# Attention over sixteen images: projections in even units, transposes in odd ones, statistics earlier

## The chip, the core and the metric

The kernel runs on one core of one Trainium2 chip. The metric is the device time of one execution in microseconds; the median of three runs before the change is 4224.94 us (4224.76 to 4225.04).

## What is computed

For each of 16 images of 1024 tokens and 512 channels: a group norm over 32 groups of 16 channels with scale and offset, SiLU, a projection to queries, keys and values (512 x 1536), attention with 8 heads of 64, an output projection (512 x 512) with bias, and the image itself added.

```
xn  = silu(group_norm(x, gn_scale, gn_offset))
q, k, v = split(xn @ w_qkv)            # 8 heads of 64, q scaled by 64 ** -0.5
out = softmax(q @ k.T) @ v             # per image and head
return out @ w_out + b_out + x
```

All of it is float32 in the reference. The kernel keeps that accuracy with pairs of float16 numbers: a value is split into a high part (rounded to float16) and a remainder (low part), and a product takes three passes (high x high, high x low, low x high).

## The kernel before

**Units.** One image is 64 units `v`, four steps `s` of 16 units `u`; a step is a pair of heads, a unit is 512 queries of one head against 256 keys. In unit `v` PE makes the scores (four matmuls of 512 columns, L1018 and L1019), ACT the exponentials twice (L591 in float32, L594 in float16), DVE (even `v`, L795) or POOL (odd `v`, L492) their remainder, and PE the product with V of unit `v - 2` (L1052). ACT takes the sums out of PSUM every fourth unit (L602), DVE and POOL normalise them (L802, L803, L499).

**Score blocks ("tops").** Before the exponentials of a head can start, each query's maximum is needed. `top_use` makes a block of raw scores with one matmul on 64 of the 128 rows (L943), DVE takes its maximum (L741), and after eight blocks a shift is computed (L731, L733) and spread over the rows by a further block (L951, L746). A unit holds three, two or one block (`TOPS_PER_W`). They go through two PSUM banks: PE's block n waits until DVE has drained block n - 2.

**Side uses.** Everything else that PE does shares one PSUM bank, SD, and is put into units by the table `SIDE`, one dictionary per step: "qk" (a half of Q or K of the next step's pair), "v" (128 tokens of V of the next image), "out" (128 tokens of the output of the image before), each 12 matmuls of 512 columns (L929); "xt" (128 tokens of the next image's x transposed, four float32 transposes, L992), "ot" (a half of the attention output of a pair transposed, L986), and "mean" and "var", two small matmuls that average channel statistics over groups (L996, L999). A side use waits until the one before it is drained: ACT writes the high part (L553, L558, L569) or the copy (L565), DVE the remainder (L682, L687, L694) or, for "out", adds bias and image (L699). ACT and DVE drain a side use at the start of the next unit (`side_before`).

**Order inside a unit on PE** (`step`, L1057 to L1082): scores; `place[0]` score blocks; the product with V; blocks up to `place[1]`; the first half of a projection ("qk", "v", "out" are split, `SPLIT`); blocks up to `place[2]`; the second half, or a whole transpose; the other blocks. `TOP_PLACES` depends on whether the unit before held a projection ("late"): (1, 2, 3) if not, (2, 2, 3) if so, and one block fewer in each eighth unit.

**The next image's statistics.** SP loads x (`load_x`, two buffers) once PE has transposed the block two before. When all eight "xt" are drained, DVE takes `bn_stats` over the channels (`channel_stats`, eight of 512 tokens, L756) and joins them (`aggregate`, L762); "mean" and "var" follow on PE with a few small DVE instructions each (L705 to L722), POOL makes three Newton steps for the reciprocal root (`newton`, twelve small instructions, L466 to L473), DVE the coefficients (`coefficients`, L770 to L780). Then the SiLU, eight pieces: ACT in units 7 to 14 of step 2 (`silu_parts`, L579 and L581), DVE one unit later (`silu`, L785 and L788), POOL the remainder (`low_xn`, L479). A "qk" of step 3 and a "v" wait for these remainders.

**SP's queue.** In order: stores of outputs, loads of the second half of the residual rows (each waits for a store), loads of x, and in unit 10 of each step `place`: 12 DMAs that copy Q and K of the next pair to where the scores read them (L385).

The loops over images run on each engine by itself; the first two steps and the last image stand outside the loop, and after the last unit an epilogue does what is left ("ot" of pairs 2 and 3 and eight "out").

Of the kernel before, what the change touches and what calls it, by code (L numbers as in the profile page):

```python
# [78 lines left out]
def top_uses(step, u, last=False):  # L79
# [3 lines left out]
    if last and step == 3 and hh == 1:  # L83
# [14 lines left out]
    {0: "qk", 1: ("ot", 2, 0), 2: "qk", 3: ("ot", 2, 1), 4: "qk", 5: "qk", 6: ("ot", 3, 0),  # L98
     7: ("ot", 3, 1), 8: "out", 10: "out", 12: "out", 13: "out", 14: "out", 15: "out"},
    {0: "qk", 1: "xt", 2: "qk", 3: "xt", 4: "qk", 5: "xt", 6: "qk", 7: "xt", 8: "xt", 9: "xt", 10: "xt",  # L100
     11: "xt", 13: "out", 14: "out"},
    {0: ("ot", 0, 0), 1: ("ot", 0, 1), 2: "mean", 3: "qk", 4: "var", 5: "qk", 6: "qk", 7: "qk", 12: "v",
     13: "v", 14: "v"},
    {0: "qk", 1: ("ot", 1, 0), 2: "qk", 3: ("ot", 1, 1), 4: "qk", 5: "qk", 8: "v", 10: "v", 12: "v",
# [10 lines left out]
def side_uses(step, u, first=False, last=False):  # L115


    kind = SIDE[step].get(u)
    if kind is None:
        return []  # L120
    if kind[0] == "ot":
        return [] if first and step == 0 else [kind]

    n = sum(k == kind for at, k in SIDE[step].items() if at < u)
    if kind == "qk":
        return [] if last and step == 3 else [("qk", (step + 1) % 4, "qk"[n % 2], n // 2)]
    if kind == "out":
        return [] if first else [("out", n + (list(SIDE[0].values()).count("out") if step == 1 else 0))]
    if last:
        return []  # L130
    if kind == "v":
        n += list(SIDE[2].values()).count("v") if step == 3 else 0
    return [(kind, n)]
# [34 lines left out]
EPILOGUE = [("ot", pair, half) for pair in (2, 3) for half in (0, 1)] + [("out", t) for t in range(TB)]  # L168
# [42 lines left out]
def conv_attention(nc, x, gamma, beta, w_qkv, w_out, b_out, out):  # L211
# [4 lines left out]
    with ctx:  # L216
# [132 lines left out]
        def _(sp):  # L349
# [36 lines left out]

            def step(b, s, cnt, first=False, last=False):
                filled = []
# [3 lines left out]
                for u in range(16):  # L392
# [10 lines left out]
                    if s == 0 and u == 9 and not last:  # L403
# [38 lines left out]
        def _(pool):  # L442
# [63 lines left out]
            def step(b, s, first=False, last=False):  # L506
                for u in range(16):
# [5 lines left out]
                    if s == 2 and u == 5 and not last:  # L513
# [133 lines left out]
        def _(dve):  # L647
# [164 lines left out]
            def step(b, s, cnt, first=False, last=False):  # L812
                for u in range(16):
# [16 lines left out]
                    if s == 1 and u >= 12 and not last:  # L830
                        channel_stats(b + 1, 2 * u - 24, cnt)
                        channel_stats(b + 1, 2 * u - 23, cnt)
                    if s == 2 and not last:
                        if u == 1:


                            aggregate(b + 1)
                        if u == 6:
# [301 lines left out]
```

## Time and profile before

| | |
|---|---|
| median of three runs | 4224.94 us |
| profiled execution | 4226.06 us |
| its span (first to last instruction) | 4224.3 us |
| PE busy | 3989.4 us (94%) |
| DVE busy | 3128.5 us (74%) |
| ACT busy | 2835.4 us (67%) |
| POOL busy | 1626.7 us (39%) |
| mean granted TensorE clock | 0.981 |

The page gives, for one execution, how long each engine was busy and who waited for whom. PE's busy time counts a matmul from its start to its modelled end, so matmuls that follow each other every 0.22 us appear with some 0.38 us each and overlap; the distance between starts says what one costs. The granted clock is 1.00 when TensorE runs at 2.4 GHz and 0.50 at 1.2 GHz. A unit is recognised by its first score matmul (L1018), and a step by sixteen of them.

### The profile page before, as it was taken

Reading aid. Unit: us, or ns where it says so; the run is one execution under the profiler, and the core shown is the slowest. Engines: PE = TensorE matmul, PEld = TensorE weight load, DVE = VectorE, ACT = ScalarE, POOL = GpSimd, SP = SyncE. Lnnn points to the kernel's source line nnn. Section 1 sums busy time; section 2 is a strip of 40 time slices with the busy share of each in tenths; the row PEclk is TensorE's granted clock in tenths of the full one; section 3 lists DMA queues with packets and bytes.
Section 4 is the critical chain, followed back from the end, with each engine's and each line's share of the span. In section 5 each row is a group of like instructions: output and inputs, shape, how many; then the busy total and the mean of one; then the engine's idle time right before and its main releaser. Section 6 shows DMA issues by size and latency. Waiting matters only on the chain.

```text
span 4224.3 us, 94104 instructions
## 1 busy us (share of the span) xinstructions
PE 3989.4 (94%) x32844; PEld 2038.7 (48%) x32844; DVE 3128.5 (74%) x5216; ACT 2835.4 (67%) x3202; POOL 1626.7 (39%) x1226
## 2 busy tenths in 40 slices
PE   3899999999999999999999999999999999999997
PEld 1444545445454444545445454454544545454443
DVE  5686777868777687776877778687776877778774
ACT  2576676767667676676766767676676766767664
POOL 1243343433434343343433434333343433434333
PEclk8999999999999999999999999999999999999999
DMA  2111212122031120311112121220311203121121
GB/s 77 28 49 36 71 31 76 31 61 61 16 91 31 51 56 19 88 31 56 51 43 68 28 76 33 59 61 16 91 31 51 56 24 83 31 59 49 39 60 33
DMA packets 119394, 211.50 MB, mean 50 GB/s; under 512 B 19536, under 2 KB 19536, under 8 KB 118992
## 3 DMA queue, kind: packets, MB, share of 16 engines
q1 hardware_dynamic: 118992, 205.86, 18.0%
q8 instruction: 286, 4.69, 0.5%
q14 instruction: 116, 0.95, 0.1%
HBM read 71.57 MB, written 33.55 MB: 25 GB/s over the span
## 4 chain that ended last, share of the span: by engine, by line
PE 71%; issue 12%; DVE 9%; POOL 4%; ACT 3%; DVEq 1%; DMA 0%; SPq 0%; ACTq 0%; POOLq 0%
PE SD L929 31%; PE PV L1052 13%; PE TP L943 10%; PE ST L1018 6%; PE ST L1019 6%; DVE Pl L795 2%; DVE mx L741 2%; POOL Pl L492 2%; PE SD L992 1%; POOL xn L479 1%; PE TP L951 1%; ACT QK_hi L553 1%; PE SD L986 1%; ACT Ph L594 1%; DVE Q L746 1%
## 5 line engine op out<-in xcount | busy, mean ns | idle before, releaser
L741 DVE TENSOR_REDUCE mx<-TP 128x1 f32<-128x512 f32 x2048 | 1349.3, 684 | 346.7 <-PE TP L943 338.1
L591 ACT ACTIVATE P<-ST,cns 128x1024 f32<-128x1024 f32 x1024 | 1142.6, 1116 | 532.6 <-PE ST L1019 484.1
L492 POOL TENSOR_TENSOR Pl<-P,Ph 128x1024 f16<-128x1024 f32 x512 | 1116.6, 2181 | 796.2 <-ACT Ph L594 796.0
L594 ACT ACTIVATE Ph<-ST,cns 128x1024 f16<-128x1024 f32 x1024 | 1138.0, 1111 | 0.0
L1052 PE MATMUL PV<-V,Ph 128*128 128x129 f16 (+2 forms) x10240 | 884.9, 212 | 43.7 <-POOL Pl L492 31.0
L1052 PEld LDWEIGHTS PV<-V,Ph 128*128 128x128 f16 x10240 | 766.6, 98 | 309.4 <-issue 271.9
L1052 PE MATMUL PV<-V,Pl 128*128 128x65 f16 x8192 | 850.1, 194 | 0.0
L943 PE MATMUL TP<-QK_hi 64*128 64x512 f16 x2048 | 722.6, 388 | 70.8 <-DVE mx L741 50.0
L1018 PE MATMUL ST<-Q,K 128*128 128x512 f16 x2048 | 785.7, 384 | 1.8 <-issue 0.2
L1019 PE MATMUL ST<-Q,K 128*128 128x512 f16 x2048 | 785.0, 383 | 0.0
L929 PE MATMUL SD<-xn,wq 128*128 128x512 f16 x3072 | 735.9, 382 | 25.3 <-POOL xn L479 16.0
L1052 PEld LDWEIGHTS PV<-V,Pl 128*128 128x128 f16 x8192 | 732.5, 99 | 3.9
L499 POOL TENSOR_TENSOR O<-pv_sum,den 128x256 f32<-128x256 f32 x256 | 169.2, 661 | 1412.0 <-DVE pv_sum L803 1407.0
L795 DVE TENSOR_TENSOR Pl<-P,Ph 128x1024 f16<-128x1024 f32 x512 | 662.0, 1293 | 8.7 <-ACT Ph L594 8.7
L553 ACT ACTIVATE QK_hi<-SD,sc 128x512 f16<-128x512 f32 x256 | 175.9, 687 | 525.7 <-PE SD L929 525.7
L682 DVE SCALAR_TENSOR_TENSOR QK_lo<-SD,sc,QK_hi 128x512 f16<-128x512 f32 x256 | 192.2, 751 | 355.9 <-ACT QK_hi L553 340.1
L929 PEld LDWEIGHTS SD<-xn,wq 128*128 128x128 f16 x3072 | 269.7, 98 | 374.5 <-issue 83.5
L943 PEld LDWEIGHTS TP<-QK_hi 64*128 64x128 f16 x2048 | 159.7, 93 | 553.1 <-issue 290.8
L929 PE MATMUL SD<-wo,OT 128*128 128x512 f16 x1536 | 363.0, 381 | 16.4 <-DVE OT L694 10.4
L929 PE MATMUL SD<-wq,xn 128*128 128x512 f16 x1536 | 364.6, 381 | 10.8 <-DVE V L687 6.5
L1018 PEld LDWEIGHTS ST<-Q,K 128*128 128x128 f16 x2048 | 203.5, 99 | 213.6 <-issue 33.5
L1019 PEld LDWEIGHTS ST<-Q,K 128*128 128x128 f16 x2048 | 201.6, 98 | 184.6 <-issue 5.0
(92 smaller groups left out, 2826.3 us busy)
## 6 DMA issues: line engine op xcount, KB each, us to landing
work<-in_x SPq DMA_DIRECT2D x128, 256.0 KB, 2.7
Q<-QK_hi SPq DMA_DIRECT2D x256, 128.0 KB, 2.7
K<-QK_hi SPq DMA_DIRECT2D x256, 128.0 KB, 2.8
res<-in_x SPq DMA_DIRECT2D x128, 256.0 KB, 3.0
out<-res SPq DMA_DIRECT2D x128, 256.0 KB, 2.3
K<-QK_lo SPq DMA_DIRECT2D x128, 128.0 KB, 2.7
Q<-QK_lo SPq DMA_DIRECT2D x128, 128.0 KB, 2.7
V<-in_L_conv_w_qkv SPq DMA_DIRECT2D x1, 3072.0 KB, 10.4
```

What stands on the lines that cost most here:

```text
L492: nc.gpsimd.tensor_tensor(Pl[:, v % 4, :], P32[:, v % 2, :], Ph[:, v % 4, :], ALU.subtract).then_inc(lo_pool, 1)
L553: nc.scalar.activation(QK_hi[:, pair % 2, i, bass.ts(half, HALF)], SD[:], ACT.Identity, scale=sc[:, col:col + 1]).then_inc(side_hi, 1)
L591: nc.scalar.activation(P32[:, v % 2, :], ST[:, v % 2, :], ACT.Exp, scale=cns[:, 0:1])
L594: nc.scalar.activation(Ph[:, v % 4, :], ST[:, v % 2, :], ACT.Exp, scale=cns[:, 0:1]).then_inc(exp_done, 1)
L682: nc.vector.scalar_tensor_tensor(out=QK_lo[:, i, cols], in0=SD[:], scalar=sc[:, col:col + 1], in1=QK_hi[:, pair % 2, i, cols], op0=ALU.mul ...
L741: nc.vector.reduce_max(mx[:, hh, qb, kh:kh + 1], TP[:, cnt.top_bank], AX.X).then_inc(top_drained, 1)
L795: nc.vector.tensor_tensor(Pl[:, v % 4, :], P32[:, v % 2, :], Ph[:, v % 4, :], ALU.subtract).then_inc(lo_dve, 1)
L929: ins = nc.tensor.matmul(SD[:], stationary(i, c), moving(j, c), start=(c == 0 and i + j == 0), stop=(c == CC - 1 and i == 1))
L943: ins = nc.tensor.matmul(TP[:, bank], QK_hi[r, pair % 2, 0, bass.ts(qb, P)], QK_hi[r, pair % 2, 1, bass.ts(kh, HALF)], start=True, stop=True)
L1018: nc.tensor.matmul(dst, K1[:, slot, kb], Q1[:, slot, bass.ts(q, HALF)], start=True, stop=False)
L1019: ins = nc.tensor.matmul(dst, K2[:, slot, kb], Q2[:, slot, bass.ts(q, HALF)], start=False, stop=True)
L1052: ins = nc.tensor.matmul(PV[:, cols], stationary, moving, start=kb == qb == n == 0, stop=kb == TB - 1, skip_group_check=True)
```

## The change

Only the places of work in the order change; the instructions of each use stay the same.

- `SIDE`: projections stand in even units (in step 3 also in units 9 and 13), transposes in odd ones. "ot" of a pair comes one step after its heads, so that of pair 2 moves from step 0 of the next image to step 3 of its own. "xt" moves from step 1 alone to the odd units 9 to 15 of step 0 and 1 to 7 of step 1. "out" stands four times in step 0 and four times in step 1 (six and two before), "v" twice in step 2 and six times in step 3 (three and five before). "mean" and "var" move from units 2 and 4 of step 2 to units 13 and 15 of step 1.
- The first two loads of x are issued in unit 6 of step 0 instead of unit 9; the list of fill counts on SP is kept from step 0 to step 1.
- DVE: `channel_stats` in units 8 to 11 of step 1 instead of 12 to 15, `aggregate` in unit 12 of step 1 instead of unit 1 of step 2, `coefficients` in unit 4 of step 2 instead of 6.
- POOL: `newton` in unit 1 of step 2 instead of 5. The SiLU keeps its places.
- The epilogue holds "ot" of pair 3 only.

```diff
 SIDE = [
-    {0: "qk", 1: ("ot", 2, 0), 2: "qk", 3: ("ot", 2, 1), 4: "qk", 5: "qk", 6: ("ot", 3, 0),
-     7: ("ot", 3, 1), 8: "out", 10: "out", 12: "out", 13: "out", 14: "out", 15: "out"},
-    {0: "qk", 1: "xt", 2: "qk", 3: "xt", 4: "qk", 5: "xt", 6: "qk", 7: "xt", 8: "xt", 9: "xt", 10: "xt",
-     11: "xt", 13: "out", 14: "out"},
-    {0: ("ot", 0, 0), 1: ("ot", 0, 1), 2: "mean", 3: "qk", 4: "var", 5: "qk", 6: "qk", 7: "qk", 12: "v",
-     13: "v", 14: "v"},
-    {0: "qk", 1: ("ot", 1, 0), 2: "qk", 3: ("ot", 1, 1), 4: "qk", 5: "qk", 8: "v", 10: "v", 12: "v",
+    {0: "qk", 2: "qk", 3: ("ot", 3, 0), 4: "qk", 5: ("ot", 3, 1), 6: "qk", 8: "out", 9: "xt", 10: "out", 11: "xt",
+     12: "out", 13: "xt", 14: "out", 15: "xt"},
+    {0: "qk", 1: "xt", 2: "qk", 3: "xt", 4: "qk", 5: "xt", 6: "qk", 7: "xt", 8: "out", 10: "out", 12: "out",
+     13: "mean", 14: "out", 15: "var"},
+    {0: "qk", 1: ("ot", 0, 0), 2: "qk", 3: ("ot", 0, 1), 4: "qk", 6: "qk", 7: ("ot", 1, 0), 9: ("ot", 1, 1),
+     12: "v", 14: "v"},
+    {0: "qk", 2: "qk", 3: ("ot", 2, 0), 4: "qk", 5: ("ot", 2, 1), 6: "qk", 8: "v", 9: "v", 10: "v", 12: "v",
      13: "v", 14: "v"},
 ]
...
+    if kind == "xt":
+        n += list(SIDE[0].values()).count("xt") if step == 1 else 0
...
-EPILOGUE = [("ot", pair, half) for pair in (2, 3) for half in (0, 1)] + [("out", t) for t in range(TB)]
+EPILOGUE = [("ot", 3, half) for half in (0, 1)] + [("out", t) for t in range(TB)]
...
-                    if s == 0 and u == 9 and not last:
+                    if s == 0 and u == 6 and not last:
                         load_x(b + 1, 0, cnt.side)
                         load_x(b + 1, 1, cnt.side)
...
-                    if s == 2 and u == 5 and not last:
+                    if s == 2 and u == 1 and not last:
                         newton(b + 1)
...
-                    if s == 1 and u >= 12 and not last:
-                        channel_stats(b + 1, 2 * u - 24, cnt)
-                        channel_stats(b + 1, 2 * u - 23, cnt)
+                    if s == 1 and 8 <= u < 12 and not last:
+                        channel_stats(b + 1, 2 * u - 16, cnt)
+                        channel_stats(b + 1, 2 * u - 15, cnt)
+                    if s == 1 and u == 12 and not last:
+                        aggregate(b + 1)
                     if s == 2 and not last:
-                        if u == 1:
-                            aggregate(b + 1)
-                        if u == 6:
+                        if u == 4:
                             coefficients(b + 1)
```

## Rows read from the trace of the kernel before

**Rows 1.** Page, busy us (share of span) and instructions of each engine.
```profile
PE 3989.4 (94%) x32844; PEld 2038.7 (48%) x32844; DVE 3128.5 (74%) x5216; ACT 2835.4 (67%) x3202; POOL 1626.7 (39%) x1226
```
**Rows 2.** Stretches (image; step 2): length, busy PE, PEld, DVE, ACT, POOL, clock, DMA.
```profile
2161.10:2417.10 256.00, 247.75 (x2058) 127.02 (x2054) 193.10 (x325) 176.69 (x201) 101.59 (x76) 0.99 0.19 51
2285.55:2352.78 67.23, 61.52 (x497) 32.00 (x497) 56.36 (x105) 52.13 (x62) 30.51 (x31) 0.95 0.17 44
```
**Rows 3.** Timeline of PE, unit 4 of step 0 and its neighbours: start, duration, work.
```profile
2177.03 0.63 PE L986 MATMUL SD<-ident,O 128*128 128x128 f32 x4
2177.49 0.38 PE L1018 MATMUL ST<-Q,K 128*128 128x512 f16 x1
...
2181.10 0.39 PE L943 MATMUL TP<-QK_hi 64*128 64x512 f16 x1
2181.42 1.47 PE L929 MATMUL SD<-xn,wq 128*128 128x512 f16 x6
2182.73 0.38 PE L1018 MATMUL ST<-Q,K 128*128 128x512 f16 x1
...
2183.38 0.38 PE L1019 MATMUL ST<-Q,K 128*128 128x512 f16 x1
2183.69 0.60 PE L943 MATMUL TP<-QK_hi 64*128 64x512 f16 x2
```
**Rows 4.** Stretches, step 2: units 7, 8 to 9, 10, 11, 12, then 13 to 15.
```profile
2313.93:2318.73 4.80, 4.55 (x39) 2.55 (x38) 3.82 (x9) 4.21 (x5) 2.13 (x2) 1.00 0.00 0
2318.73:2324.61 5.88, 5.18 (x52) 2.58 (x49) 4.33 (x8) 5.37 (x7) 1.13 (x2) 1.00 0.44 103
2324.61:2329.62 5.01, 2.87 (x26) 1.34 (x26) 4.97 (x9) 5.01 (x7) 2.56 (x3) 1.00 0.73 169
2329.62:2334.04 4.42, 3.29 (x25) 1.84 (x25) 4.32 (x8) 3.07 (x4) 3.26 (x3) 0.73 0.14 32
2334.04:2341.40 7.36, 7.26 (x42) 3.69 (x42) 5.53 (x8) 5.05 (x7) 3.47 (x3) 0.70 0.00 1
2341.40:2352.78 11.38, 11.38 (x100) 5.91 (x98) 10.47 (x19) 10.24 (x13) 6.55 (x5) 1.00 0.01 1
sum 38.85, PE 34.53 PEld 17.91 DVE 33.44 ACT 32.94 POOL 19.09; mean PE 5.75 PEld 2.99 DVE 5.57 ACT 5.49 POOL 3.18
```
**Rows 5.** Waits in units 8 to 12 of step 2: total us, times, longest.
```profile
PE TP L943 <- DVE mx L741: 1.6, 1, 1.6
```
**Rows 6.** Groups of DVE instructions, thirteen images: busy us, mean ns; idle before.
```profile
L687 DVE SCALAR_TENSOR_TENSOR V<-SD,sc,V 128x512 f16<-128x512 f32 x104 | 78.3, 753 | 108.4 <-ACT V L558 108.4
L694 DVE TENSOR_TENSOR OT<-SD,OT 128x512 f16<-128x512 f32 x104 | 71.1, 684 | 15.1 <-ACT OT L569 12.4 <-DVE mv L762 2.7
L756 DVE BATCH_NORM_STATS2 st<-work 128x6 f32<-128x512 f32 x104 | 66.6, 682 | 0.4
```
**Rows 7.** Stretches: units 8 to 11 of step 0; units 0 to 2 of step 2.
```profile
2192.56:2208.67 16.11, 15.40 (x124) 7.13 (x122) 12.60 (x21) 9.03 (x11) 6.09 (x3) 1.00 0.23 73
2285.55:2296.02 10.47, 9.35 (x85) 5.21 (x86) 9.67 (x21) 8.91 (x11) 4.62 (x3) 1.00 0.40 123
```
**Rows 8.** Timelines of DVE and POOL, the coefficients in unit 6 of step 2.
```profile
2312.41 0.15 DVE L770 TENSOR_TENSOR gn<-gam,gn 128x4 f32<-128x4 f32 x1
2312.60 1.98 DVE L772 TENSOR_TENSOR gn<-gn 128x4 f32<-128x4 f32 x1
...
2315.38 0.75 DVE L682 SCALAR_TENSOR_TENSOR QK_lo<-SD,sc,QK_hi 128x512 f16<-128x512 f32 x1
...
2312.43 2.13 POOL L492 TENSOR_TENSOR Pl<-P,Ph 128x1024 f16<-128x1024 f32 x1 [0.22 <-ACT Ph L594]
```
**Rows 9.** Timeline of SP's queue, first and last placement DMA in step 0.
```profile
2210.53 0.47 SPq L385 DMA_DIRECT2D Q<-QK_hi  x1
...
2217.44 0.60 SPq L385 DMA_DIRECT2D K<-QK_hi  x1
```
**Rows 10.** Timeline of DVE in the epilogue, a remainder of "ot"; idle before it in brackets.
```profile
4184.60 0.69 DVE L694 TENSOR_TENSOR OT<-SD,OT 128x512 f16<-128x512 f32 x1 [1.91 <-ACT OT L569]
```

More of the change, by code:

```diff
@@ L385, in place @@
                         sp.dma_start(dst, src).then_inc(placed[hh], 16)
+            filled = []
             def step(b, s, cnt, first=False, last=False):
-                filled = []
+                if s == 0:
+                    filled.clear()
                 if s == 2:
```

## Prediction

> **What bounds the kernel now.** I read the page's busy shares first, then the table of stretches for one image and its second-last step, then TensorE's timeline for the price of a unit, then the table of stretches again unit by unit. The reader is to see two regimes. Over the span PE is busy 94% and DVE 74% [rows 1]; one image takes 256.0 us, PE busy in 247.75 of it [rows 2]. But nearly all of PE's open time lies in step 2: 61.52 busy of 67.23 us there, 5.7 of the image's 8.3 us [rows 2]. Cut that step at each unit's first score matmul and it is clear where: in units 10 and 11 PE is busy 2.87 of 5.01 and 3.29 of 4.42 us, while DVE is busy 4.97 of 5.01 and 4.32 of 4.42 [rows 4]. Those units carry no projection; each carries a piece of the silu (two ACT passes, two DVE passes) on top of the usual exponentials and maxima. The waits say the same: PE's longest wait there is for DVE's maximum, 1.6 us [rows 5]. So PE sets the time everywhere except in the silu stretch, units 7 to 15 of step 2, where DVE (with ACT close to it) does.
>
> The dip of TensorE's clock stands there too: the granted clock is 0.73 in unit 11 and 0.70 in unit 12, right after PE idled in unit 10, which means part of the time at 1.2 instead of 2.4 GHz [rows 4]. Unit 12 (three score blocks and a projection) takes 7.36 us; a warm unit with the same contents takes 5.24 (2177.49 to 2182.73) [rows 3, 4]. So the dip costs 2.1 us there and somewhat less than 1 in unit 11, where DVE waits anyway.
>
> **The change, part by part; per image first.** The arithmetic is the same, so I price only order.
>
> (a) Groups of score blocks. A score block matmul uses 64 of the 128 rows, and entering and leaving a run of them costs extra: the step from L1019 to L943 is 0.31 us (2183.38 to 2183.69) and from L943 to L929 0.32 (2181.10 to 2181.42), where matmuls of the same length in a run come every 0.22 (six take 1.47, the last 0.38 of it) [rows 3]. That is 0.19 us for each separate run. The order (split or not, late or not) gives 97 runs in an image before and 102 after, counted over the 64 units (a unit behind a projection takes its first two blocks as one run, and fewer units with two or three loose blocks stand there now). +0.95 us, on PE, uncovered except in the silu stretch. Little uncertainty.
>
> (b) The silu stretch. Units 7 to 15 lose two projections (the last "qk" of unit 7, the "v" of unit 13), 12 x 0.217 = 2.6 us each, and get two transposes ("ot" in 7 and 9), 0.46 each (2177.03 to 2177.49) [rows 3]. So 4.2 us of PE work leave the one stretch where PE waits, and stand in the units of the other steps where PE never waits: +4.2 there. What the stretch gives back depends on DVE. It lasts 38.85 us, DVE busy 33.44 of it (the sum of its rows) [rows 4]. Its DVE work afterwards: two "ot" remainders more (0.68 each), one QK remainder and one V remainder less (each 0.75, L687's form): 33.3 us, unchanged [rows 6]. PE work is then about 27 us, so DVE alone decides. If DVE ran at the 98.5% of units 10 and 11 (9.29 of 9.43) throughout, 33.8 us; if nothing is given back, 38.85. In units 8 to 11 it ran at 89% (13.62 of 15.31) [rows 4], because it also waits for PE's blocks and ACT's halves, and unit 7 is now so short (about 2.3 against 4.80 us) that its ACT and DVE work runs on into unit 8. I take 93%, between the two, 35.9 us, which includes that the clock dip costs less when PE is not what is waited for. -3.0 + 4.2 = +1.2 us; ends -0.85 and +4.2.
>
> (c) Statistics and coefficients. Before, eight bn_stats stand in units 12 to 15 of step 1 and their backlog falls on units 0 to 2 of step 2, which carry only transposes and "mean": PE idles 1.1 us there (9.35 of 10.47) [rows 7]. That goes. What is late next: the statistics now stand in units 8 to 11 of step 1, which have projections in 8 and 10 like units 8 to 11 of step 0. Those take 16.11 us with DVE busy 12.60 [rows 7]; add 8 x 0.68 (L756) and take off the one "ot" remainder, 0.68 [rows 6]: 17.4 us of DVE work in 16.11, 1.3 us too much. The next shift block (unit 12) waits for DVE's last maximum, so this shows on PE. Units 12 to 15 have room, so it ends there. The coefficients move from unit 6 to 4, ahead of a unit without a side use. Before, this chain took DVE from 2312.41 to 2315.38, and 1.98 us of that is one 128x4 product that lasts as long as POOL's L492 beside it (2.13 us) [rows 8]. So it costs between 1 and 3 us of DVE time in either place; I keep it even. POOL's Newton steps move from unit 5 to 1; behind them stands the remainder of unit 1's probabilities, wanted only two units later, and units 1 and 2 are now 8 us long: nothing. Net (c): +0.2; ends -1.1 (hidden) and +2.2 (if the next shift is caught as well).
>
> The trace fits a rule of the Trainium skill (SBUF — State Buffer, "SBUF: two separate sides"): VectorE and GpSimd share a port pair as an exclusive lock, and the loser blocks for the whole instruction. By that rule the product would drop to some 0.2 us once it no longer meets L492, and (c) would be near -1; the trace shows the meeting, not that unit 4 avoids it.
>
> (d) x's transposes. The eight "xt" go from step 1 into odd units of steps 0 and 1, where a transposed unit follows a projection, as units 1 and 3 do now: 0.46 us each as before. Their drain is one ACT pass. On SP's queue the loads of x now stand between stores and placements: the twelve placement DMAs take from 2210.53 to 2218.04 [rows 9], the load for the fourth block is behind them, and unit 15 of step 0 wants it. After a placement that starts in unit 12 and ends early in unit 14 about 3 us are left: nothing, but see the rivals.
>
> (e) Once: "ot" of pair 2 leaves the tail, where each half costs a full round PE, ACT, DVE: 1.91 idle and 0.69 busy on DVE, 2.60 us [rows 10]. Two fewer is -5.2; the first one left now waits for the last normalisation, about +1.2: -4.
>
> Sum per image: 0.95 + 1.2 + 0.2 = +2.35; ends -1.0 and +7.3. Fifteen images prepare a successor: +35. With (e), 4226.06 (the profiled execution, 1.8 over its span) + 35 - 4 = 4257. The profiled execution is 1.1 above the median of the runs, so **4256 us**, its own range 4234 to 4278.
>
> **Rivals.**
> - Faster: the silu stretch falls to 33.8 us because DVE really is all that counts and the dip goes with the two long units; the statistics hide. Place: units 7 to 15 of step 2; it decides below about 34.7 us. 0.95 - 0.85 - 1.1 = -1.0 per image: 4226.06 - 15 - 4 - 1.1 = 4206. For it: DVE at 98% in units 10, 11. Against: 89% over units 8 to 11, and PE's spare work has left.
> - No change: the stretch at 34.9 us (+0.25), statistics hidden (-1.1): +0.1 per image, 4222 to 4226.
> - The statistics bind: (c) at its upper end, +2.0 more per image: 4286. For it: 17.4 us of DVE work in 16.1; against: DVE has slack on either side.
> - A longer or second clock dip: PE idles more between units 7 and 13 than now. Priced by unit 12, 2.1 us per image: 4287. Against: where PE waits for DVE, a slow PE costs less. The Trainium skill (TensorE: Matmul & The Clock Gate, "HAM oscillation — how this bites in real kernels") says that repeated micro-idling between groups of matmuls makes the clock fall back again and again; before, rows show one dip per silu stretch, so by that rule this case would be the likely one.
> - SP's queue: if placements run late, the fourth x block is late in unit 15 of step 0; 2 us per image: 4286.
>
> **How the numbers follow.** Forecast 0.47, statistics 0.12, second dip 0.11, SP 0.05, no change 0.12, faster 0.13. A change within 0.2% (8.4 us) cannot be told from none: 4216.5 to 4233.4. Slower 0.75, same 0.12, faster 0.13. The range runs from 4215 to 4288: it leaves out the faster case and the ends in which the stretch gives nothing back (about 4300).
>
> **What would show it.** Units 8 to 11 of step 2 with DVE at 90% or more and PE well under 70% busy; the nine units 7 to 15 near 36 us; the other steps with PE nearly without idle time, step 3 longest by the moved "v". The clock table: one dip per image. Wrong if the stretch is under 34.7 us, or if units 8 to 12 of step 1 show more than 2 us of PE idle. (a) is wrong if warm units of the same contents cost the same whatever the number of runs.

## The result and the profile after

The changed kernel takes 4301.96 us (median of four runs, 4299.38 to 4302.91) against 4224.99 before (4224.76 to 4225.89): a ratio of 1.0181, 95% interval 1.0163 to 1.0198, 77 us slower. The forecast had the direction, but 31 us in place of 77, and the time lies above the range. The profiled execution took 4299.38 us, its span is 4297.6, which is 73.3 more than before.

The page of the kernel after, first part: busy time, share of the span and instructions of each engine.

```profile
PE 4005.4 (93%) x32844; PEld 2024.8 (47%) x32844; DVE 3215.9 (75%) x5216; ACT 2823.4 (66%) x3202; POOL 1621.7 (38%) x1226
```

Against [rows 1] the numbers of instructions are the same, but DVE is busy 87 us longer; the last section comes back to that. Steady images take 260.7 us in place of the 256.0 of [rows 2]. The 73.3 us of the span split so: prologue +0.2, first image +8.25 (241.04 to 249.29), the next fourteen +68.0 together, last image and epilogue -3.15.

The table says where in a steady image it goes. It is the mean of twelve images (2 to 13). "Open" is the length less a sum over the stretch's matmuls: for each pair in succession the shortest step between their starts (tenth percentile) that such a pair shows at full clock in the traces. It holds the waits and what a slow clock costs.

| stretch (step, units) | before us | open | after us | open |
|---|---|---|---|---|
| 0, all | 66.82 | 1.93 | 62.48 | 1.57 |
| 1, 0 to 7 | 31.31 | 0.60 | 31.53 | 0.63 |
| 1, 8 to 15 (statistics) | 26.37 | 0.88 | 31.81 | 2.22 |
| 2, 0 to 6 (coefficients) | 28.39 | 2.29 | 30.47 | 2.22 |
| 2, 7 to 15 (silu) | 38.82 | 8.13 | 36.13 | 9.53 |
| 3, 0 to 2 | 13.84 | 0.51 | 15.04 | 2.14 |
| 3, 3 to 15 | 50.46 | 2.41 | 53.30 | 2.24 |
| image | 256.00 | 16.75 | 260.76 | 20.54 |

Of the 4.76 us, 0.97 are order (length less "open" rises from 239.25 to 240.22) and 3.8 are waits.

Stretches of the kernel after in step 2, units 7, 8, 9, 10, 11, 12, then 13 to 15: length, busy PE, PEld, DVE, ACT, POOL, clock, DMA.

```profile
2359.57:2361.84 2.27, 2.27 (x32) 1.78 (x31) 1.34 (x2) 1.89 (x3) 0.00 (x0) 1.00 0.00 0
2361.84:2366.35 4.51, 2.79 (x27) 1.34 (x25) 2.80 (x5) 4.51 (x6) 2.13 (x1) 1.00 0.76 176
2366.35:2370.51 4.16, 4.16 (x30) 2.68 (x29) 4.12 (x7) 4.16 (x7) 1.16 (x1) 0.65 0.81 188
2370.51:2374.41 3.90, 3.04 (x26) 1.42 (x25) 3.87 (x9) 3.90 (x7) 2.49 (x3) 0.94 0.02 4
2374.41:2377.42 3.01, 2.47 (x25) 1.26 (x25) 2.91 (x7) 2.58 (x5) 1.85 (x2) 1.00 0.00 0
2377.42:2385.53 8.11, 5.48 (x41) 2.66 (x41) 6.35 (x9) 5.78 (x7) 4.29 (x3) 1.00 0.00 1
2385.53:2395.63 10.10, 9.25 (x88) 4.79 (x86) 9.55 (x17) 9.58 (x12) 5.39 (x4) 1.00 0.01 2
sum 36.06, PE 29.47 PEld 15.93 DVE 30.94 ACT 32.41 POOL 17.30; mean PE 4.21 PEld 2.28 DVE 4.42 ACT 4.63 POOL 2.47
```

The sum answers to that of [rows 4]: 36.06 us against 38.85, as forecast (35.9). But DVE's busy time in it fell with the length, from 33.44 to 30.94, where the forecast had it unchanged: it is no fuller than before, 86% in both. And the longest unit, 12, is not DVE's: 6.35 busy of 8.11 us. Nor is unit 8, where ACT is busy without a gap (4.51 us, as in units 9 and 10) and DVE only 2.80. PE waits 1.7 us there for DVE's maximum, but DVE had idled just as long (idle before in brackets) for ACT's copy of the transpose of unit 7, which stands behind the passes of the silu:

```profile
2364.68 0.69 DVE L699 TENSOR_TENSOR OT<-SD,OT 128x512 f16<-128x512 f32 x1 [1.71 <-ACT OT L574]
```

The forecast priced the two transposes of this stretch on PE and on DVE, not this wait.

Stretches, unit 0 and then units 1 and 2 of step 3, after:

```profile
2395.63:2402.31 6.68, 5.56 (x42) 2.43 (x40) 6.07 (x9) 3.31 (x4) 3.48 (x3) 1.00 0.00 0
2402.31:2410.66 8.35, 7.71 (x63) 3.56 (x62) 5.92 (x11) 5.26 (x6) 5.66 (x5) 1.00 0.01 2
```

and the same three units in one stretch, before:

```profile
2352.78:2366.61 13.83, 13.67 (x107) 6.46 (x105) 11.19 (x19) 9.14 (x11) 8.07 (x7) 1.00 0.00 1
```

PE had 0.16 us open there before and has 1.76 after (6.68 - 5.56 and 8.35 - 7.71). The timeline of DVE across the border of the steps (start, duration, work) shows why. Before, where step 3 begins at 2352.78: the shift of unit 15, the remainder of unit 14, the end of the last piece of the silu.

```profile
2349.29 1.21 DVE L733 TENSOR_SCALAR ms<-mx,cns 128x4 f16<-128x4 f32 x1
...
2352.58 1.29 DVE L795 TENSOR_TENSOR Pl<-P,Ph 128x1024 f16<-128x1024 f32 x1
...
2355.35 0.43 DVE L788 CAST xn<-work 128x512 f16<-128x512 f32 x1
```

After, where it begins at 2395.63:

```profile
2392.71 1.92 DVE L738 TENSOR_SCALAR ms<-mx,cns 128x4 f16<-128x4 f32 x1
...
2396.26 1.74 DVE L800 TENSOR_TENSOR Pl<-P,Ph 128x1024 f16<-128x1024 f32 x1
...
2399.48 0.43 DVE L793 CAST xn<-work 128x512 f16<-128x512 f32 x1
```

Before, the silu ends 3.00 us behind the border (2355.78), after 4.28 (2399.91). DVE is 0.57 us later at the shift (2.92 us ahead of the border in place of 3.49), and the shift and the remainder take 1.16 us longer; 0.45 us is made up between. PE's product in unit 0 needs that remainder, and its wait for it is 1.1 us.

The second new place is unit 3 of step 2. Stretches of units 0 to 2, 3, and 4 to 6, after:

```profile
2329.10:2342.89 13.79, 13.69 (x102) 6.47 (x103) 10.81 (x21) 8.00 (x10) 4.90 (x13) 1.00 0.33 94
2342.89:2346.80 3.91, 2.74 (x30) 1.60 (x29) 2.98 (x3) 1.92 (x3) 2.32 (x2) 1.00 0.00 0
2346.80:2359.57 12.77, 12.55 (x102) 6.21 (x100) 10.59 (x23) 8.65 (x10) 4.83 (x3) 1.00 0.01 1
```

The 1.1 us that PE idled in units 0 to 2 [rows 7] are gone, as the statistics left. In unit 3, 1.17 us are open instead. POOL's timeline, what stands ahead of the twelve Newton steps, their first and last, and what stands behind (idle before in brackets):

```profile
2339.29 0.62 POOL L504 TENSOR_TENSOR O<-pv_sum,den 128x256 f32<-128x256 f32 x1 [7.78 <-DVE pv_sum L808]
2339.87 0.20 POOL L471 TENSOR_TENSOR nt<-gn 128x4 f32<-128x4 f32 x1
...
2342.93 0.20 POOL L478 TENSOR_TENSOR gn<-gn,nt 128x4 f32<-128x4 f32 x1
2343.36 2.12 POOL L497 TENSOR_TENSOR Pl<-P,Ph 128x1024 f16<-128x1024 f32 x1 [0.23 <-POOL gn L478]
```

The steps hold up the remainder of unit 1's probabilities (L497) by 3.5 us, from 2339.87 to 2343.36; PE wants it in unit 3, which begins at 2342.89. The waits of PE in this image, after (total us, times, longest); the wait of [rows 5] stands in the first row, 1.7 in place of 1.6:

```profile
PE TP L946 <- DVE mx L746: 4.2, 6, 1.7
PE PV L1055 <- DVE Pl L800: 2.0, 2, 1.1
PE PV L1055 <- POOL Pl L497: 1.7, 2, 1.2
PE SD L932 <- POOL xn L484: 1.7, 1, 1.7
...
```

### The profile page after: what moved, and what is told of

It is laid out like the page before. It is cut to its first block, busy times and chain, and to the rows that moved or that the text cites. A ratio compares the mean times of both kernels' runs of the same rounds, so it can differ in the third digit from the quotient of the medians.

```text
span 4297.6 us, 94105 instructions
## 1 busy us (share of the span) xinstructions
PE 4005.4 (93%) x32844; PEld 2024.8 (47%) x32844; DVE 3215.9 (75%) x5216; ACT 2823.4 (66%) x3202; POOL 1621.7 (38%) x1226
## 4 chain that ended last, share of the span: by engine, by line
PE 63%; issue 18%; DVE 8%; POOL 7%; ACT 3%; DVEq 0%; POOLq 0%; DMA 0%; SPq 0%; ACTq 0%
PE SD L932 28%; PE PV L1055 12%; PE TP L946 9%; PE ST L1022 5%; PE ST L1021 5%; POOL Pl L497 5%; DVE mx L746 3%; DVE Pl L800 2%; POOL xn L484 1%; PE SD L995 1%; PE TP L954 1%; ACT QK_hi L558 1%; PE SD L989 1%; ACT Ph L599 1%; ACT V L563 1%
## 5 line engine op out<-in xcount | busy, mean ns | idle before, releaser
L497 POOL TENSOR_TENSOR Pl<-P,Ph 128x1024 f16<-128x1024 f32 x512 | 1116.3, 2180 | 854.7 <-ACT Ph L599 851.3
L946 PE MATMUL TP<-QK_hi 64*128 64x512 f16 x2048 | 733.8, 389 | 81.3 <-DVE mx L746 77.7
L800 DVE TENSOR_TENSOR Pl<-P,Ph 128x1024 f16<-128x1024 f32 x512 | 681.3, 1331 | 8.7 <-ACT Ph L599 8.7
L932 PE MATMUL SD<-wq,xn 128*128 128x512 f16 x1536 | 365.2, 381 | 21.9 <-POOL xn L484 13.5
L932 PE MATMUL SD<-wo,OT 128*128 128x512 f16 x1536 | 371.9, 382 | 7.5 <-DVE res L704 5.9
L1021 PEld LDWEIGHTS ST<-Q,K 128*128 128x128 f16 x2048 | 202.4, 99 | 210.8 <-issue 33.3
## 6 DMA issues: line engine op xcount, KB each, us to landing
work<-in_x SPq DMA_DIRECT2D x128, 256.0 KB, 2.8
res<-in_x SPq DMA_DIRECT2D x128, 256.0 KB, 3.2
out<-res SPq DMA_DIRECT2D x128, 256.0 KB, 2.0
```

Of the source, the lines that this page charges most:

```text
L497: nc.gpsimd.tensor_tensor(Pl[:, v % 4, :], P32[:, v % 2, :], Ph[:, v % 4, :], ALU.subtract).then_inc(lo_pool, 1)
L800: nc.vector.tensor_tensor(Pl[:, v % 4, :], P32[:, v % 2, :], Ph[:, v % 4, :], ALU.subtract).then_inc(lo_dve, 1)
L932: ins = nc.tensor.matmul(SD[:], stationary(i, c), moving(j, c), start=(c == 0 and i + j == 0), stop=(c == CC - 1 and i == 1))
L946: ins = nc.tensor.matmul(TP[:, bank], QK_hi[r, pair % 2, 0, bass.ts(qb, P)], QK_hi[r, pair % 2, 1, bass.ts(kh, HALF)], start=True, stop=True)
L1021: nc.tensor.matmul(dst, K1[:, slot, kb], Q1[:, slot, bass.ts(q, HALF)], start=True, stop=False)
```

## The experiments

**Newton steps one unit later** (from the changed kernel; they then stand behind the remainder of unit 1).

```diff
-                    if s == 2 and u == 1 and not last:
+                    if s == 2 and u == 2 and not last:
                         newton(b + 1)
```

> The changed kernel with POOL's Newton steps in unit 2 of step 2, behind the remainder of unit 1's probabilities instead of ahead of it. Theory: in the changed kernel PE waits 1.2 us per image for that remainder in unit 3 of step 2, because twelve small POOL instructions stand ahead of it; with them behind it the wait goes and nothing else moves: 15 x 1.2 = 18 us less, 4284 us. Rival: the wait only passes on, to the coefficients in unit 4 or to unit 8, where DVE is late anyway: 4298 to 4303.

4279.31 us, ratio to before 1.0132 (1.0115 to 1.0149), 22.7 less than after. Unit 3 of step 2:

```profile
2330.68:2333.36 2.68, 2.68 (x29) 1.59 (x28) 1.76 (x2) 2.30 (x3) 2.13 (x8) 1.00 0.00 0
```

The 1.2 us are gone (units 0 to 6: open 2.22 to 0.99), every other stretch is unchanged within 0.1. The theory held (18 us were expected).

**A projection back into unit 13 of the silu stretch** (from the changed kernel).

```diff
-     12: "v", 14: "v"},
-    {0: "qk", 2: "qk", 3: ("ot", 2, 0), 4: "qk", 5: ("ot", 2, 1), 6: "qk", 8: "v", 9: "v", 10: "v", 12: "v",
+     12: "v", 13: "v", 14: "v"},
+    {0: "qk", 2: "qk", 3: ("ot", 2, 0), 4: "qk", 5: ("ot", 2, 1), 6: "qk", 8: "v", 10: "v", 12: "v",
```

> The changed kernel with the projection v back in unit 13 of step 2 (and out of unit 9 of step 3). Theory: units 7 to 15 of step 2 are bound by DVE, so 2.6 us of PE work cost nearly nothing there and leave step 3, where PE binds; DVE gets one 0.75 us remainder more inside the stretch. Net 1 to 2 us less per image: 4272 to 4287 us. Rival: PE pays for the projection wherever it stands (the loss came from runs of score blocks and from the clock): 4300 +- 4. Second rival: ACT and DVE are so far behind at unit 13 that the extra drain lengthens the stretch by all it gained elsewhere: 4302 or slower.

4269.61 us (1.0103, 1.0086 to 1.012), 32.4 less than after and a little more than the theory had. Units 0 to 2 of step 3, which begin at 2382.25, and DVE's shift ahead of them:

```profile
2382.25:2396.01 13.76, 13.14 (x104) 6.00 (x102) 10.69 (x18) 8.65 (x10) 8.00 (x7) 1.00 0.00 1
```

```profile
2378.76 1.21 DVE L738 TENSOR_SCALAR ms<-mx,cns 128x4 f16<-128x4 f32 x1
```

In the mean the silu stretch grows by 1.45 us (36.13 to 37.58) for 2.6 us of work, units 8 to 15 of step 3 lose 2.10, and units 0 to 2 of step 3 lose 1.28 (15.04 to 13.76): the backlog is gone. At the border DVE stands where it stood in the kernel before (shift 3.49 us ahead of it in 1.21 us, remainder in 1.29, silu ended 3.00 behind, each the mean of twelve images). So the short unit 13 of the change is paid behind the border.

**Statistics spread thinner**: four of the eight `bn_stats` in units 1, 3, 5 and 7 of step 1, one each in units 8 to 11.

```diff
+                    if s == 1 and u in (1, 3, 5, 7) and not last:
+                        channel_stats(b + 1, u - 1, cnt)
                     if s == 1 and 8 <= u < 12 and not last:
-                        channel_stats(b + 1, 2 * u - 16, cnt)
                         channel_stats(b + 1, 2 * u - 15, cnt)
```

> The changed kernel with the bn_stats spread: the four over the first half of the tokens stand in units 1, 3, 5, 7 of step 1, the four over the second half in units 8 to 11, one per unit. Theory: eight of 0.68 us in units 8 to 11 are more than DVE can take beside its usual work; one per unit fits, and 1.3 us of waits in units 8 to 15 of step 1 go: 4282 us. Rival: units 1 to 7 of step 1 have no room either, the waits only move: 4302.

4293.57 us (1.0164, 1.0147 to 1.0181), 8.4 less, under half of what was expected. Units 8 to 15 of step 1 fall from 2.22 to 1.62 open: the shift block of unit 12 no longer waits, that of unit 15 still does. The statistics cause the first of the two waits only, and the silu stretch takes 0.27 us of the gain back (36.13 to 36.40).

**Less DVE work in the silu**: of the cast of each piece seven eighths of the columns are left out (all images but the first).

```diff
-                nc.vector.tensor_copy(xn[:, 0, c, tokens], xT[:, c, tokens]).then_inc(xn_hi, 1)
+                part = tokens if isinstance(image, int) and image == 0 else bass.ts(i // CC * 8, HALF // 8)
+                nc.vector.tensor_copy(xn[:, 0, c, part], xT[:, c, part]).then_inc(xn_hi, 1)
```

> The changed kernel with the second DVE pass of the silu (the cast to the float16 high part) over an eighth of its columns, for every image but the first: part of the normalised image is left out, nothing else. It takes some 0.4 us of DVE work from each of units 8 to 15 of step 2 and nothing from PE, ACT or POOL. Theory (DVE binds this stretch and its backlog runs into step 3): 2.5 to 3.3 us less per image, 4253 to 4265 us. Rival (ACT binds it, with 3.4 us of passes per unit): at most 0.7 us per image, 4291 to 4302.

4280.84 us (1.013, 1.0113 to 1.0147), 21 less, between the theory and the rival. The stretch falls by 0.72 only, units 0 to 2 of step 3 by 0.43. Waits of PE in unit 12 of step 2:

```profile
PE SD L933 <- POOL xn L484: 1.5, 1, 1.5
PE PV L1056 <- DVE Pl L801: 1.2, 1, 1.2
```

In this unit the first projection of the next image waits for POOL's remainder of the silu; less DVE work doesn't bring it sooner (the unit takes 8.10 us in place of 8.11). In unit 8 DVE idles the same 1.71 us for ACT as with the whole cast. So the amount of DVE's work doesn't set the stretch alone: ACT does in unit 8, and in unit 12 the order of a piece through DVE and POOL, where a "v" needs it.

**The first three together.**

> The changed kernel with the three edits at once: Newton steps in unit 2 of step 2, v back in unit 13, bn_stats spread over units 1, 3, 5, 7 and 8 to 11 of step 1. Theory: three separate places (POOL ahead of unit 3, the silu stretch with its backlog into step 3, DVE in step 1), so the single gains of 22.7, 32.4 and 8.4 us add up: 4302 - 63.5 = 4238 us, within 6. Rival: the places are coupled through DVE's backlog or the clock's dip, and half of it or less adds: 4250 to 4265.

4244.76 us (1.0041, 1.0025 to 1.0058): 57.2 less than after, where the three singly add to 63.5: nearly the theory, 0.8 us outside its 6. The image takes 257.12 us.

**And the silu one unit earlier on ACT, DVE and POOL** (from the one before).

```diff
-                    if s == 2 and 7 <= u < 15 and not last:
-                        silu_parts(b + 1, u - 7)
+                    if s == 2 and 6 <= u < 14 and not last:
+                        silu_parts(b + 1, u - 6)
...
-                        if u >= 8:
-                            silu(b + 1, u - 8)
+                        if 7 <= u < 15:
+                            silu(b + 1, u - 7)
```

> The three edits, and the silu one unit earlier on ACT, DVE and POOL (ACT in units 6 to 13 of step 2, DVE and POOL in 7 to 14), so that its first pieces lie beside the projection of unit 6. Theory: the silu's units are bound by ACT, DVE and POOL, so a unit with 2.6 us of projection beside them costs nothing more and one bare unit behind it loses its wait: 1.5 to 2.5 us less per image than the three edits alone, 4200 to 4216 us, which is under the kernel before. Rival: what counts is the chain to the fourth remainder of the normalised image, for which unit 12 waits 1 to 1.8 us; it moves earlier and that wait alone goes: 4211 to 4223. Second rival: DVE is so late in unit 7 that unit 8 loses the same: 4238.

4231.24 us (1.0009, 0.9993 to 1.0025), 13.5 less, not the 29 or more of the theory, and between its two rivals. PE's waits in units 7 to 15 of step 2, first with the silu in its old place, then earlier:

```profile
PE TP L947 <- DVE mx L746: 1.7, 1, 1.7
PE SD L933 <- POOL xn L484: 1.7, 1, 1.7
PE PV L1056 <- DVE Pl L800: 1.2, 1, 1.2
```

```profile
PE TP L947 <- DVE mx L746: 2.7, 2, 1.7
PE PV L1056 <- DVE Pl L800: 0.9, 1, 0.9
PE PV L1056 <- POOL Pl L497: 0.5, 1, 0.5
...
```

The wait for POOL's xn is gone; a second wait for DVE's maximum and one for POOL's Pl stand in its place.

**"qk" back in unit 7** (from the three together; "ot" of pair 1 in unit 6).

```diff
-    {0: "qk", 1: ("ot", 0, 0), 2: "qk", 3: ("ot", 0, 1), 4: "qk", 6: "qk", 7: ("ot", 1, 0), 9: ("ot", 1, 1),
+    {0: "qk", 1: ("ot", 0, 0), 2: "qk", 3: ("ot", 0, 1), 4: "qk", 6: ("ot", 1, 0), 7: "qk", 9: ("ot", 1, 1),
```

> The three edits, and the last qk of step 2 back in unit 7 with the transpose of unit 7 in unit 6: one projection more beside the silu, 2.6 us. Theory: as it costs nothing there, 1 to 2 us less per image than the three edits alone, 4208 to 4223 us. Rival: its remainder on DVE stands ahead of unit 8's blocks, as in the kernel before, where unit 8 waits 0.8 us for it; nothing is left: 4235 to 4240.

4237.18 us (1.0025, 1.0009 to 1.0041), 7.6 less: the rival. Units 0 to 6 take 2.10 us less, the stretch 1.60 more, and the wait for QK's remainder in unit 8 (0.7 us) is back, as it was before the change.

**The kernel before with its statistics spread** (one `bn_stats` in each of units 8 to 15 of step 1).

```diff
-                    if s == 1 and u >= 12 and not last:
-                        channel_stats(b + 1, 2 * u - 24, cnt)
-                        channel_stats(b + 1, 2 * u - 23, cnt)
+                    if s == 1 and 8 <= u and not last:
+                        channel_stats(b + 1, 2 * u - 16 if u < 12 else 2 * u - 23, cnt)
```

> The kernel before (not the changed one) with its bn_stats spread, one per unit over units 8 to 15 of step 1 instead of two per unit over 12 to 15. Theory: the waits in unit 15 of step 1 and units 0 to 2 of step 2 (0.3, 0.6 and 0.9 us) go in the main: 1.0 to 1.7 us per image, 4199 to 4210 us. Rival: every steady image of the kernel before lasts 256.0 us to 0.03 and the clock dips at the same place in each; a shorter way to the silu stretch moves the stretch against the clock, the dip costs more, and the image stays at 256.0: 4221 to 4226.

4224.93 us (0.9993, 0.9978 to 1.0009). Units 0 to 6 of step 2 lose 0.54, units 8 to 15 of step 1 gain 0.36: the theory was wrong, most of the backlog only changes its place. A steady image takes 255.75 us (255.71 to 255.82), so the rival's 256.0 isn't met either; the time doesn't show the 0.25 us, since in the profiled execution the second last image took 264.75 us in place of 259.40.

**Fewer runs of score blocks** (from the changed kernel; 80 in place of 102 in an image).

```diff
-TOP_PLACES = [[(1, 2, 3), (2, 2, 3)], [(0, 1, 3), (1, 1, 3)]]
+TOP_PLACES = [[(2, 2, 3), (2, 2, 3)], [(0, 1, 3), (1, 1, 3)]]
```

> The changed kernel with score blocks placed (2, 2, 3) in every unit but the eighths, so that the first two blocks are one run also where no projection stands ahead: 80 separate runs per image instead of 102. Theory (a run's entry and exit cost 0.19 us of PE): 22 x 0.19 = 4.2 us per image, 63 us in all, 4239 us if PE waits for nothing new; PE then comes to its second block sooner than DVE drains, which gives some back: 4239 to 4270. Rival: blocks that stand together wait for DVE, and all is given back: 4295 to 4305.

4357.91 us (1.0313, 1.0296 to 1.033), 56 more: wrong by the sign. PE's own order falls by 4.14 us an image (240.22 to 236.08), which is 22 x 0.19: in the distances between starts the price of a run is there. But open time rises from 20.5 to 28.6. Waits of PE in one image:

```profile
PE TP L946 <- DVE mx L746: 7.8, 14, 1.8
PE TP L946 <- DVE Q L751: 2.9, 4, 1.8
...
```

Blocks that stand apart leave DVE time to drain a bank before it is wanted again; joined, they wait 14 times in place of 6. A run's price buys that time.

The clock adds to it. Unit 12 of step 2 and units 0 to 2 of step 3 in that image (the clock is the third number from the end):

```profile
2407.87:2418.84 10.97, 8.38 (x46) 3.37 (x43) 7.27 (x11) 6.18 (x8) 4.72 (x4) 0.69 0.00 1
...
2428.88:2446.12 17.24, 14.66 (x104) 6.72 (x102) 11.91 (x20) 8.57 (x10) 9.31 (x7) 0.90 0.00 1
```

Between the two the clock is 1.00, so these are separate dips. Twelve images have 28 dips here and 14 in the kernel after, and the clock is low for 8.8 us an image in place of 6.0.

**POOL's bias additions out of units 0 to 3 of step 3** (into units 8 to 11; from the kernel with the earlier silu).

```diff
-                    if s == 3 and u < 4:
-                        add_bias(b, u)
+                    if s == 3 and 8 <= u < 12:
+                        add_bias(b, u - 8)
```

> The kernel with the three edits and the silu one unit earlier (4231 us), and POOL's bias additions of step 3 in units 8 to 11 instead of 0 to 3. Theory: the waits in units 0, 2 and 4 of step 3 (0.4, 0.6 and 1.1 us) come from POOL's work beside DVE's small instructions there; 1 to 2 us per image, 4201 to 4216 us, under the kernel before. Rival: they are DVE's own backlog of the silu, and stay: 4226 to 4233.

4233.47 us (1.0016, 1.0006 to 1.0025): nothing gained. Units 3 to 7 lose 1.13 us of waits and units 8 to 15 gain 1.14, now in unit 12. DVE's timeline there, and under it POOL's:

```profile
2401.38 2.35 DVE L800 TENSOR_TENSOR Pl<-P,Ph 128x1024 f16<-128x1024 f32 x1
```

```profile
2400.15 2.50 POOL L489 TENSOR_TENSOR res<-res,bias 128x512 f32<-128x512 f32 x2
```

DVE's remainder takes 2.35 us beside POOL's additions, where without them it takes 1.22; what followed it, the maxima that the next shift needs, is late. The edit only moves the meeting.

**Fewer runs of score blocks in that kernel** (the same edit of `TOP_PLACES` as above).

> As the run with the silu earlier and the bias additions moved, with score blocks placed (2, 2, 3) as in the changed kernel's run of that kind. Theory: runs of score blocks cost PE the same here, so it gains what that run gains against the changed kernel, within 15 us. Rival: with fewer bare units DVE is tighter and PE waits for its maxima: no gain.

4272.24 us (1.0108, 1.0091 to 1.0125), 39 more than without it: the same answer.

**A fourth "v" in the silu stretch** (in unit 11; from the kernel with the silu earlier and the bias additions in units 8 to 11).

```diff
-     12: "v", 13: "v", 14: "v"},
+     11: "v", 12: "v", 13: "v", 14: "v"},
...
-     13: "v", 14: "v"},
+     14: "v"},
```

> As the run with the silu earlier and the bias additions moved, and a fourth v in step 2 (unit 11) instead of step 3 (unit 13): 2.6 us more of PE work beside the silu. Theory: the stretch costs nearly the same, so 1 to 2 us per image less than that run: 15 to 30 us under it. Rival: the silu's first four remainders are only just there in unit 11, PE waits for them, and nothing or less is gained.

4228.69 us (1.0004, 0.9994 to 1.0013): 4.8 less than that kernel, where 15 to 30 were expected. The stretch grows by 2.10 us and step 3 loses 2.09 behind its unit 2, so the fourth "v" is paid in full; units 0 to 2 of step 3 lose 0.36. The image takes 256.00 us in the mean.

**And the bias additions in units 5, 7, 13 and 15**:

```diff
-                    if s == 3 and 8 <= u < 12:
-                        add_bias(b, u - 8)
+                    if s == 3 and u in (5, 7, 13, 15):
+                        add_bias(b, (5, 7, 13, 15).index(u))
```

> The repaired kernel with four v in step 2 (4228.7 us), with POOL's four bias additions of step 3 in units 5, 7, 13 and 15 instead of 8 to 11. There a wait of 1.6 us per image stands in unit 12 of step 3 for the shift; with the additions in units 0 to 3 it stood in unit 4 (1.1 us). Theory: DVE's small instruction for the shift, in units 2 and 10, is held up by POOL's additions; away from there the wait falls to the 0.5 us it had anyway: 1.1 us x 15 = 16 us less, 4212 us, under the kernel before. Rival: the clock's dip gives it back, 4224 to 4229.

4226.02 us (1.0000, 0.9991 to 1.0009). Units 8 to 15 of step 3 lose 1.13 us as foreseen (31.73 to 30.60), yet the image stays at 256.00 in the mean, as the rival had it: the silu stretch grew by 1.04 (38.67 to 39.71), though nothing in it was edited. Its units 7 to 10 and 11 in one image, fourth "v" only:

```profile
2316.52:2331.86 15.34, 13.63 (x109) 7.69 (x107) 13.03 (x21) 14.60 (x19) 7.25 (x6) 0.78 0.45 104
2331.86:2338.45 6.59, 5.15 (x38) 2.46 (x38) 6.45 (x11) 4.87 (x6) 2.53 (x2) 1.00 0.01 1
```

and units 7 to 9, 10 and 11 with the additions moved as well:

```profile
2315.70:2325.39 9.69, 7.98 (x85) 4.86 (x84) 8.05 (x13) 9.31 (x12) 4.06 (x3) 1.00 0.62 144
2325.39:2330.68 5.29, 2.85 (x28) 1.33 (x25) 5.26 (x9) 5.29 (x8) 2.84 (x4) 1.00 0.17 38
2330.68:2338.98 8.30, 8.09 (x37) 3.42 (x37) 6.66 (x11) 4.77 (x6) 4.32 (x4) 0.59 0.00 1
```

In these two images the dip of the clock has moved from units 7 to 10, where PE waits anyway, to unit 11 with its "v" (clock 0.59, 8.30 us in place of 6.59). Over twelve images it stands in unit 11 in all, where it did in three; some 0.7 of the 1.04 us are slower matmuls (by the difference to full-clock steps). The kernel with the fourth "v" alone shows the price as well: two of its three images with the dip in unit 11 take 257.21 and 257.37 us, the nine without 255.59 to 255.88; in the third the dip is half as long (255.64).

**The bias additions alone, in the kernel before** (the same edit as in the last).

> The kernel before with the same edit: bias additions of step 3 in units 5, 7, 13, 15 instead of 0 to 3. Theory: the wait of 1.05 us per image in unit 4 of step 3 goes: 15 us less, 4210 us. Rival: the steady image stays at 256.0 us because the silu stretch then meets the clock's dip at another place and pays for it: 4221 to 4226.

4220.65 us (0.9989, 0.998 to 0.9998): 5 us less than before and 81 less than after, the only kernel here whose interval lies (barely) below before. That is a third of the theory's 15 us. The rival's reason fails too: a steady image takes 255.43 us (255.41 to 255.45), and the silu stretch 38.74 in place of 38.82. DVE's remainder ahead of unit 4 of step 3 is back at its short time, where it took 2.27 us before:

```profile
2363.67 1.22 DVE L795 TENSOR_TENSOR Pl<-P,Ph 128x1024 f16<-128x1024 f32 x1
```

PE's wait of 0.9 us in unit 4 is gone, and a shorter one stands in unit 7:

```profile
PE PV L1052 <- POOL Pl L492: 0.5, 1, 0.5
```

## Why the prediction was wrong, by its own steps

Per steady image, forecast and measured:

| term | forecast | measured |
|---|---|---|
| (a) runs of score blocks, 97 to 102 | 0.95 | 0.97 |
| (b) silu stretch, waits | 1.2 | 1.40 |
| (b) what runs on behind unit 15 | not priced | 1.63 |
| (c) statistics and coefficients | 0.2 | 0.04 (+1.34 in step 1, -1.30 in step 2) |
| (c) Newton steps ahead of unit 1's remainder | 0 | 1.23 |
| elsewhere | 0 | -0.50 |
| sum | 2.35 | 4.77 |

**The failed steps.** The first is in (b), "so DVE alone decides", with the account closed at unit 15. The length came out (36.1 against 35.9), but by luck: DVE fills 86% of it and not 93, and its work there is 30.94 us and not 33.3. Of the 2.4 us, 1.5 are the coefficients, which in the kernel before ended in unit 7 and which the change itself moves out; 0.9 are the remainders of unit 14 (of "v" and of the probabilities), which now fall behind unit 15. For short units let PE reach step 3 before DVE: units 0 to 2 of step 3 lose 1.63 us, more than the 1.2 that the stretch was to cost. The projection put back into unit 13 takes 1.28 of it away. Nor is it DVE alone: unit 8 waits for ACT and unit 12 for POOL, and with less DVE work in every piece the stretch shortens by 0.7 us only. The sign named for it failed as well: in units 8 to 11 DVE is busy 88%, where 90 or more was named, and PE 80%, where it was to be well under 70. DVE's 1.28 us at the border are 0.57 by which it is late at the shift and 1.16 by which two instructions take longer, less the 0.45 made up.

The second is in (c), "wanted only two units later, and units 1 and 2 are now 8 us long: nothing". Counted from the unit's start that holds; but POOL starts the steps at 2339.87, late in unit 2, since its normalisation ahead of them waits for DVE until 2339.29. The twelve steps take 3.5 us and the remainder 2.1, to 2345.48, and unit 3 begins at 2342.89. The experiment with one unit later gives back 22.7 us.

Together they are 2.86 of the 4.77 us, more than the 2.4 by which the forecast falls short in a steady image. Outside these images two more things were off: the first took 8.25 us longer, not 2.35 (it has no output projections to fill its units; with the three repairs and the earlier silu it is back at 241.03 us, and what is due to which wasn't studied), and the last image with the epilogue gave -3.15, not the -4 of (e).

**Right.** (a), by the count, by the difference of order, and by the order in the experiment with fewer runs. (c)'s trade of the statistics. (d): no wait for x or for a placement appears among PE's waits.

**Rivals.** The statistics bound at 1.34 us in units 8 to 15 of step 1, paid back in step 2. SP's queue didn't show. A second dip of the clock didn't decide. Two of the twelve images have two dips, but the clock is low for 6.0 us an image after against 6.8 before, and slow matmuls cost 0.3 to 0.4 us less than before, by the difference to full-clock steps. Nor does its place decide here: the dip stands in units 9 and 10 (as in the image shown), in 11 and 12, or half in each, and every image takes 260.67 to 261.05 us. The Trainium skill's rule of repeated micro-idling (TensorE: Matmul & The Clock Gate, "A second HAM failure mode: psum-queue depth-cycling"; the prediction names the section ahead of it) would have had the dips grow, since PE waits in units 8, 10, 11 and 12. The trace of the kernel after doesn't agree (6.0 us against 6.8); that of the changed kernel with fewer runs does (8.8 us, with 14 waits for maxima in place of 6).

**What stays open.** The three repairs bring 57 us, the earlier silu 13.5, the rest 5: the repairs and the earlier silu each remove the wait that they are aimed at, and what comes later gains less and less. Projections in even units are thus no gain in any form tried (4226.02 at best), and why the time comes back is shown for one pair of kernels only (the dip moved to a costlier unit, some 0.7 of 1.04 us). That three kernels have a mean image of 256.00 us may have one cause or none: it wasn't found.

## What to carry to other kernels

A stretch that gets shorter has only gained if the engine that bounded it ends no later: compare its busy time in the stretch, and look into the units behind it for what is left. When instructions move on an in-order queue, count from when that engine comes free to when the one behind them is wanted, however small they are. A projection beside work that another engine bounds can cost less than its price: the third "v" of the silu stretch cost 1.45 of its 2.6 us there and took 1.28 off the units behind, the fourth cost 2.10. So take such cover away last, and expect less from each further piece.

## What the runs showed of the hardware

**DVE instructions as long as POOL's.** DVE's 87 us more come from unchanged instructions. Groups of DVE instructions with a 128x4 result in the kernel after (count, busy us, mean ns, idle before):

```profile
L738 DVE TENSOR_SCALAR ms<-mx,cns 128x4 f16<-128x4 f32 x256 | 162.6, 635 | 9.2
...
L714 DVE TENSOR_TENSOR gn<-gn 128x4 f32<-128x4 f32 x16 | 30.9, 1933 | 0.6
L723 DVE TENSOR_SCALAR gn<-gn 128x4 f32<-128x4 f32 x16 | 20.6, 1286 | 0.5
...
L777 DVE TENSOR_TENSOR gn<-gn 128x4 f32<-128x4 f32 x16 | 2.6, 163 | 0.6
```

The coefficients' product (L777), 1.98 us beside POOL in [rows 8] and 1753 ns in the mean, takes 163 ns in its new unit; but the square in "mean" (L714), 163 ns before, now takes 1933 (from 2323.42 for 2.05 us, beside a remainder of POOL's from 2323.33 for 2.13 us), and the shift (L738) went from 485 to 635. By the rule drawn on in the prediction (the Trainium skill, SBUF — State Buffer, "SBUF: two separate sides") this is the lock. The trace agrees: 140 of the 256 shifts are lengthened after and 99 before, and each of them starts inside an instruction of POOL's and ends 0.02 to 0.03 us behind its end; a lengthened remainder (L800) ends 1.08 us behind it. Moving the work moved the meeting.

**What a dip costs depends on its place.** With the fourth "v", and with the additions moved as well, unit 11 with its projection takes 6.6 to 6.7 us where its granted clock is 0.75 or more, and 8.3 to 8.8 where it is 0.59 to 0.61. In the kernel after, the dip stands in units 9 and 10 or in 11 and 12 with no more than 0.4 us between images.

**The mean of 256.00 us is no fixed length.** Before, every steady image takes 255.97 to 256.03 us. With the fourth "v" single images take 255.59 to 257.37 and with the additions moved as well 254.58 to 256.89, in a cycle of four, and only the mean is 256.00; with its statistics spread or its additions moved the kernel before takes 255.75 and 255.43.
